# The state part of an update on the whole TensorE array: eight block-diagonal 128x128 matmuls, moved behind the right sides

## The reference

```python
def step(S, inp):                       # two steps for each token
    g, a_t, b_t, k_t, v_t, q_t = inp
    bS = jnp.einsum('bhk,bhkv->bhv', b_t, S)
    S = jnp.exp(g)[..., None] * S + a_t[..., None] * bS[:, :, None, :] + k_t[..., None] * v_t[:, :, None, :]
    o = jnp.einsum('bhk,bhkv->bhv', q_t, S)
    return (S, o)
...
y = out * jax.nn.sigmoid(gate)          # then an RMS norm per head, and y @ Wo
x = _layernorm(x + attention(x))
x = _layernorm(x + x @ W + b + x @ (up_aux @ (lora_up @ (lora_down @ down_aux))))
```

## Time and profile before

| | us |
|---|---|
| median of 3 runs | 2623.15 |
| lowest and highest of them | 2622.76, 2631.74 |
| span of the profiled execution, first to last instruction | 2622.0 |
| TensorE, matmuls busy | 2288.4 (87%) |
| TensorE, weight loads busy | 1721.9 (66%) |
| VectorE busy | 1601.7 (61%) |
| ScalarE busy | 1618.0 (62%) |
| GpSimd busy | 458.8 (17%) |

### The profile page before, as it was taken

The page is one execution under the profiler, slowest core; times in us unless marked ns, Lnnn a source line. Parts: engine busy times, 40 slices in busy tenths (PEclk is TensorE's granted clock), DMA queues, the critical chain, the costliest instruction groups (busy, mean ns, idle before and its releaser), DMA issues.

```text
span 2622.0 us, 225147 instructions
## 1 busy us (share of the span) xinstructions
PE 2288.4 (87%) x102472; PEld 1721.9 (66%) x102472; DVE 1601.7 (61%) x3940; ACT 1618.0 (62%) x3048; POOL 458.8 (17%) x555
## 2 busy tenths in 40 slices
PE   6788898999988899998999998989999988999785
PEld 2556666666666666666676666666666666766573
DVE  2456366666556676656666665666666566666533
ACT  3556466666666666656666666666666666666543
POOL 1011111111111111111111111111111111111210
PEclk7879899999999999999999999999999999999987
DMA  3244455534555554455554455555445555534541
GB/s 95 74 110 121 110 148 148 141 104 127 145 141 151 137 141 111 132 138 146 144 137 118 124 145 146 148 141 142 113 129 143 145 148 148 136 103 132 140 125 41
DMA packets 692934, 338.90 MB, mean 129 GB/s; under 512 B 551794, under 2 KB 651728, under 8 KB 692816
## 3 DMA queue, kind: packets, MB, share of 16 engines
q1 hardware_dynamic: 692816, 337.67, 48.2%
HBM read 35.57 MB, written 16.78 MB: 20 GB/s over the span
## 4 chain that ended last, share of the span: by engine, by line
PE 86%; issue 10%; DVE 2%; ACT 1%; DMA 1%; SPq 0%; ACTq 0%; DVEq 0%
PE bank L570 14%; PE bank L733 13%; PE bank L712 11%; PE bank L704 8%; PE bank L724 7%; PE bank L716 5%; PE bank L593 5%; PE bank L683 5%; PE bank L622 5%; PE bank L643 3%; PE bank L577 3%; PE bank L694 2%; PE bank L602 2%; PE bank L587 2%; PE bank L584 2%
## 5 line engine op out<-in xcount | busy, mean ns | idle before, releaser
L473 POOL TENSOR_TENSOR state<-moved,edge 128x512 f32<-128x512 f32 x252 | 292.3, 1160 | 1821.9 <-DVE moved L1093 1821.9
L712 PE MATMUL bank<-parts,w_now 32*32 32x64 f32 x16512 | 420.1, 223 | 4.8 <-DMA w_now<-w_row 3.6
L570 PE MATMUL bank<-x_col,w_kqv 128*128 128x512 f32 x768 | 370.6, 619 | 48.5 <-issue 47.9
L856 ACT ACTIVATE parts<-bank,cf 128x256 f32<-128x256 f32 x512 | 214.6, 470 | 319.5 <-DVE o_col L1087 310.7
L716 PE MATMUL bank<-aq_now,delta 32*32 32x16 f32 x16512 | 403.7, 179 | 9.2 <-issue 9.2
L716 PEld LDWEIGHTS bank<-aq_now,delta 32*32 32x32 f32 x16512 | 391.7, 110 | 6.7 <-issue 6.7
L712 PEld LDWEIGHTS bank<-parts,w_now 32*32 32x32 f32 x16512 | 377.2, 110 | 17.1 <-issue 5.0
L733 PE MATMUL bank<-uq_now,s_now 32*32 32x24 f32 x32768 | 362.2, 189 | 14.5 <-issue 14.4
L733 PEld LDWEIGHTS bank<-uq_now,s_now 32*32 32x32 f32 x32768 | 337.1, 107 | 24.1 <-issue 18.2
L1116 DVE COPY_PREDICATED aq<-ci,bank 128x128 f32<-128x128 int32 x256 | 77.1, 301 | 410.3 <-PE bank L704 276.7
L1087 DVE TENSOR_TENSOR o_col<-qs,bank 128x64 f32<-128x64 f32 x512 | 89.5, 216 | 388.6 <-PE bank L716 384.7
(11 more groups left out here) (99 smaller groups left out, 3814.1 us busy)
## 6 DMA issues: line engine op xcount, KB each, us to landing
s_now<-state SPq DMA_DIRECT2D x256, 256.0 KB
uq_now<-uqv SPq DMA_DIRECT2D x256, 192.0 KB
t_now<-t_t SPq DMA_DIRECT2D x256, 128.0 KB, 2.0
w_now<-w_row SPq DMA_DIRECT2D x256, 128.0 KB
uq_a<-uqv SPq DMA_DIRECT2D x64, 384.0 KB
low<-uqv SPq DMA_DIRECT2D x64, 384.0 KB
x_col<-in_xt_dram SPq DMA_DIRECT2D x32, 512.0 KB, 5.8
w_a<-w_col SPq DMA_DIRECT2D x64, 256.0 KB
```

The source lines that it names most:

```text
L473: pool.tensor_tensor(state[:, qc, :, :, :].rearrange("p m b v -> p (m b) v"), moved[m % 2][:, :, :, :].rearrange("p m b v -> p (m b) v"), ...
L570: mm = pe.matmul(ps[:, :], w_kqv[:, a, w, f * P:(f + 1) * P], x_col[:, a, :], start=a == 0, stop=a == KT - 1)
L712: pe.matmul(ds_bank[quarter(h), m, :, :].rearrange("p b v -> p (b v)"), w_now[quarter(h), m, :], parts[quarter(h), m, :, :].rearrange("p b ...
L856: act.activation(parts[:, :, b, :], p2_bank, ACT.Copy, scale=cf[:, C_TAKE + b:C_TAKE + b + 1])
```

## The change

Seven edits that belong together:

1. `updates` keeps only the state part. For each of the 8 tiles one matmul with a 128x128 weight, in which the four heads' 32x32 blocks stand on the diagonal and the rest is zero, takes the place of four with 32x32 weights. The 32 answer matmuls become `answers`.
2. A slot runs deltas, answers, right sides, updates. Signals change with it: p3_filled becomes o_filled and ds_filled, the deltas wait for t_now and aq_now (second_in) and for qs, the right sides for first_in, the updates for s_added, w_in and parts_made.
3. w_now becomes [128, 128, 8]: row, weight column, tile. The weight of tile m is w_now[:, :, m], every eighth float. w_row is laid out as [128, chunk, 32, 8] and is written by four transposes with that stride, in place of two contiguous ones.
4. SyncE loads the diagonal with four transfers of 32 partitions by 1 KB (`stage_diagonal`), issued last in the iteration, in place of one of 128 partitions.
5. parts is no longer made by two ScalarE copies from PSUM, but by one GpSimd multiply of delta by the mask columns (`parts_part`), ahead of the decay of the same iteration.
6. inv is cleared and its diagonals set by GpSimd (five memsets) in place of ScalarE's copy of a constant; the constant is gone, and prod shares the space of uq_a's first buffer.
7. VectorE takes the answers first, then turns the right sides, then adds the state.

```diff
             def stage_first(c, n):
 
-                sp.dma_start(uq_now[:, :, :], of_chunks(uqv[c][:, :, 0:HF * UQ], n)).then_inc(uq_in.handle, 16)
-                sp.dma_start(s_now[:, :, :, :], state[:, n % QC, :, :, :]).then_inc(s_in.handle, 16)
+                sp.dma_start(uq_now[:, :, :], of_chunks(uqv[c][:, :, 0:HF * UQ], n)).then_inc(first_in.handle, 16)
+                sp.dma_start(s_now[:, :, :, :], state[:, n % QC, :, :, :]).then_inc(first_in.handle, 16)
+
+            def stage_diagonal(rows, m):
+
+                for h in range(HPH):
+                    sp.dma_start(w_now[quarter(h), quarter(h), :], rows[quarter(h), m, :, :]).then_inc(w_in.handle, 16)
...
+            def parts_part(j, n):
+
+                if not (there(j) and not (isinstance(j, int) and j * CH + n == 0) or (there(j - 1) and n < 1)):
+                    return
+                shape = [P, CT, GB, HD]
+                pool.wait_ge(ds_filled.handle, ds_filled.at(j, n + 1))
+                pool.wait_ge(delta_ready.handle, delta_ready.at(j, n))
+                pool.tensor_tensor(parts[:, :, :, :], delta[:, :, :].unsqueeze(2).to_broadcast(shape),
+                                   cf[:, C_TAKE:C_TAKE + GB].unsqueeze(1).unsqueeze(3).to_broadcast(shape),
+                                   ALU.mult).then_inc(parts_made.handle, 1)
...
             def updates():
 
                 for m in range(CT):
-                    for h in range(HPH):
-                        pe.matmul(ds_bank[quarter(h), m, :, :].rearrange("p b v -> p (b v)"), w_now[quarter(h), m, :],
-                                  parts[quarter(h), m, :, :].rearrange("p b v -> p (b v)"),
-                                  start=True, stop=True)
+                    mm = pe.matmul(ds_bank[:, m, :, :].rearrange("p b v -> p (b v)"), w_now[:, :, m],
+                                   parts[:, m, :, :].rearrange("p b v -> p (b v)"), start=True, stop=True)
+                mm.then_inc(ds_filled.handle, 1)
+
+            def answers():
+
+                for m in range(CT):
                     for h in range(HPH):
                         mm = pe.matmul(o_bank[quarter(h), m, :], delta[quarter(h), m, :], aq_now[quarter(h), m, :],
                                        start=True, stop=True)
-                mm.then_inc(p3_filled.handle, 1)
+                mm.then_inc(o_filled.handle, 1)
...
                 pe.wait_ge(set_up.handle, N_SET_UP)
-                pe.wait_ge(x_turned.handle, turn)
-                pe.wait_ge(t_in.handle, turn16)
-                pe.wait_ge(delta_ready.handle, turn)
-                pe.wait_ge(o_added.handle, turn)
+                pe.wait_ge(second_in.handle, turn32)
+                pe.wait_ge(qs_copied.handle, turn)
                 deltas()
+                answers()
 
                 pe.wait_ge(set_up.handle, N_SET_UP)
-                pe.wait_ge(w_in.handle, turn16)
-                pe.wait_ge(aq_in.handle, turn16)
+                pe.wait_ge(first_in.handle, turn32)
+                right_sides()
+
                 pe.wait_ge(s_added.handle, turn)
+                pe.wait_ge(w_in.handle, turn64)
+                pe.wait_ge(parts_made.handle, turn)
                 updates()
-
-                pe.wait_ge(set_up.handle, N_SET_UP)
-                pe.wait_ge(uq_in.handle, turn16)
-                pe.wait_ge(s_in.handle, turn16)
-                pe.wait_ge(qs_copied.handle, turn)
-                right_sides()
...
             def delta_part(j, n):
 
-                act.wait_ge(p3_filled.handle, p3_filled.at(j, n + 1))
+                act.wait_ge(parts_made.handle, parts_made.at(j, n - 1))
+                act.wait_ge(o_filled.handle, o_filled.at(j, n + 1))
                 act.wait_ge(o_added.handle, o_added.at(j, n - 1))
-                for b in range(GB):
-                    act.activation(parts[:, :, b, :], p2_bank, ACT.Copy, scale=cf[:, C_TAKE + b:C_TAKE + b + 1])
                 act.activation(delta[:, :, :], p2_bank, ACT.Copy).then_inc(delta_ready.handle, 1)
...
                 def turn_part(n):
                     if there(j):
                         turn_right_sides(j, c, n)
+                    add_state(j, n)
```

More of the change, by code:

```diff
@@ L34 @@
 C_TAKE = C_HEADS + P
-C_EYE = C_TAKE + GB
-C_EPS = C_EYE + ROWS * ROWS
+C_EPS = C_TAKE + GB
 C_LOAD = C_EPS + 5
@@ L146, in delta_block @@
         w_col = sb("w_col", [P, TILES, HD])
-        w_row = [sb(f"w_row{c}", [P, TILES, HD]) for c in range(2)]
+        w_row = [sb(f"w_row{c}", [P, CH, HD, CT]) for c in range(2)]
         gate = [sb(f"gate{c}", [P, HF, TOK]) for c in range(2)]
@@ L165, in delta_block @@
         t_now = sb("t_now", [P, CT, HD])
-        w_now = sb("w_now", [P, CT, HD])
+        w_now = sb("w_now", [P, HPH * HD, CT])
         parts = sb("parts", [P, CT, GB, HD])
@@ L381, in iteration @@
                         sp.wait_ge(p2_filled.handle, left)
[L382 to L387, removed]
+                        sp.dma_start(t_now[:, :, :], chunk(t_t, n)).then_inc(second_in.handle, 16)
+                    behind = (there(j) or (there(j - 1) and n < 1)) and not (isinstance(j, int) and j * CH + n == 0)
+                    g, m, own = (j, n - 1, c) if n >= 1 else (j - 1, CH - 1, 1 - c)
+                    if behind:
+                        left, masked = held(sp, first, o_filled.at(j, n + 1)), held(sp, second, aq_masked.at(g, CH))
                         if m == 0:
                             sp.wait_ge(aq_masked.handle, masked)
[L390 to L396, removed]
+                        sp.wait_ge(o_filled.handle, left)
+                        sp.dma_start(aq_now[:, :, :], chunk(aq[own], m)).then_inc(second_in.handle, 16)
                     if there(j) and not (isinstance(j, int) and j == G - 1 and n == CH - 1):
@@ L408, in iteration @@
                         stage_first(0, 0)
+                    if behind:
+                        left, turned = held(sp, first, ds_filled.at(j, n + 1)), held(sp, second, w_turned.at(g, 1))
+                        if m == 0:
+                            sp.wait_ge(w_turned.handle, turned)
+                        sp.wait_ge(ds_filled.handle, left)
+                        stage_diagonal(w_row[own], m)
                     if there(j + 1) and n == 0:
@@ L1088, in update, with add_state @@
                 last.then_inc(o_added.handle, 1)
+            def add_state(j, n):
+                if not scanned(j, n):
+                    return
+                g, m = (j, n - 2) if n >= 2 else (j - 1, CH + n - 2)
+                mine = state[:, m % QC, :, :, :]
+                dve.wait_ge(ds_filled.handle, ds_filled.at(j, n + 1))
                 if isinstance(g, int) and g == G - 1 and m > QC + 1:
@@ L1151, in scan_part @@
                 def scan_part(n):
-                    if there(j) and not (isinstance(j, int) and j * CH + n < 2) or (there(j - 1) and n < 2):
-                        update(j, c, n)
+                    take_answers(j, n)
                 def turn_part(n):
```

86 lines of the change are left out of this document (52 added, 34 removed).

## The result

The changed kernel takes 3618.66 us (median of 4 runs, 3615.04 to 3620.66), the kernel before 2625.88 on the same chip (median of 4, 2622.76 to 2631.74). The ratio is 1.3783 [1.3741, 1.3825]: 38% slower. Forecast was 2716 us with a range up to 2850. The sign was right, the size was not.

The account below looks back on a forecast made before the run. Bound: TensorE's own instructions plus stretches waiting for nothing visible. Per group +2.5 (slots) +0.8 (slot 5) -0.4 (slot 0) = +2.9 us; 32 groups +93; 2622.0 + 1.15 + 93 = 2716 us, own range 2675 to 2770, 80% range 2550 to 2850.

Parts of the forecast that it names:

- 16 x 0.107 = 1.71: New state matmuls on TensorE: 16 load records a slot, spaced 0.107 us apart, take 1.71 us.
- rival 1: Column-strided weight read of w_now costs extra: loads 0.203 us apart, 394 us more, 3110 us; chance 0.15.
- the two products of 0.22: VectorE's solve products: 60 elements read 64 bytes apart take 0.22 us, no more than along the row; evidence against strided cost.
- The slot at the low clock: Slot beginning at 1324.69, at 1.2 GHz: start of deltas to dense work grows by 0.30 us, from 5.39 to 5.69.
- Slot 5's wait: TensorE's second sum of squares waits for the bank that VectorE's first h_row addition drains: stall 0.8 us per group.
- the old wait of 0.45 is covered: -0.4: Slot 0, first scores waiting for uq_a: TensorE arrives 2.3 us late, VectorE 1.8, so 0.4 us per group is saved.
- 1.8 late: VectorE's delay by slot 0: solve tail starts about 1.2 us later in slot 4, plus 0.6 idle in slot 5.
- The issue piece: TensorE's queue walking branches before the dense part, 0.65 us a slot on average: hidden after the change, costed at nothing.
- Rival 3: Issue piece not hidden: a third to all of 0.65 us stays, +55 to +166 us; chance 0.13 shared with Rival 4.
- Rival 2: Loads are not the pace: some 0.055 us a record, -1.9 us per group, 2562 us; chance 0.16.
- Rival 4: w_now lands about 1.3 us late around slots 7 and 0: +42, 2758 us; chance 0.13 shared with Rival 3.
- GpSimd's product: GpSimd's added 128x512 multiply for parts: 1.16 us, done before it is needed, costing nothing; without cover about 1.2 a slot.

Follow-up runs that it names:

- Experiment 2: The changed kernel with weights read at every second or every fourth float of w_now instead of every eighth (wrong numbers, same work): 2853.07 and 3612.57 us.
- Experiment 3: contig with each of the eight state matmuls issued twice in a row: 3257.25 us.
- contig: The changed kernel with w_now and w_row stored tile by tile, so one matmul's 128 weight columns lie side by side: 2877.93 us, ratio to before 1.0971.
- experiment 7: contig with VectorE's state addition moved back, later in iterations 4, 5 and 7: 2788.33 us, ratio to before 1.0608.
- experiment 5: Masked deltas made by two ScalarE copies instead of GpSimd's product: on contig 2797.74 us; with 32x32 state matmuls (quarters_scalar) 2660.83 us.
- experiments 4 to 6: contig with 32x32 state matmuls (2683.95 us; strided weights 2674.52), with ScalarE's masked deltas (2797.74; with 32x32 matmuls too, 2660.83), or with 64x64 state matmuls (2663.65).
- quarters_scalar: contig with the state part as 32 matmuls of 32x32 and the masked deltas made by ScalarE instead of GpSimd: 2660.83 us, ratio to before 1.0137.

## Why the prediction was wrong, step by step

**The step that failed is "16 x 0.107 = 1.71", the spacing of the weight loads.** The prediction took it from two loads of contiguous columns and applied it to columns eight floats apart. It measured 0.25 a record (4.00 a block), more than double. Put into the prediction's own sum, 256 x (4.00 - 1.71) = 586 us: 2716 would have been 3302. This is rival 1, which had a chance of 0.15 and a price of 0.203, taken from ScalarE's 1133 against 597 ns, and 0.25 is dearer than that price too. The argument against it, the two products of 0.22, was VectorE's: another engine, and instructions of 60 elements. It said nothing about a weight load of 128 columns. Experiment 2 shows the mechanism as a step: nearly free at two floats apart, full price at four.

The Trainium skill, "SBUF — State Buffer", section "Door 1: The DMA port swizzle", asks for at least two hits on a 16-byte line. The trace agrees: 215 ns at two hits, 328 to 334 at one. The same place calls floats up to four apart free; the measurement contradicts it for the weight load, where four apart, one hit a line, paid in full (3612.57 us).

**The clock was left out of the sum.** It was taken as 2.4 GHz but for one slot. In the changed kernel it is at 0.50 in much of the dense work, and by the busy times this is most of the 317 us that the corrected 3302 still lacks: removing the stride took 368 us off TensorE's work outside the new matmuls, 67 of which came back as waits. Experiment 3 shows that the block's length alone isn't the cause.

**What is left without the stride** is contig's 162 us above 2716. In one group of its trace the eight slots are 5.6 longer than before, where 2.9 were forecast:
- From the slot's start to dense work 4.52 were forecast; contig shows 1509.52 - 1504.92 = 4.60. Deltas, answers and right sides are 0.65, 0.6 and 1.44 (forecast 0.68, 0.70, 1.33), the block 1.93 for 1.71. With 64 moving columns between them, loads come 0.12 apart, not 0.107.
- The slot at the low clock was given +0.30, on the argument that only the part at its start is slow. Its block takes 3.61 and the dense part 4.48: +1.8. A load at 0.226 where 0.12 is usual was nowhere in the sum.
- Slot 5's wait was forecast as 0.8 and measures 1.32 (from the end of the block at 1532.28 to the end of the addition at 1533.60). Right in place and kind; experiment 7 takes it away.
- Slot 0: "the old wait of 0.45 is covered: -0.4". It became 1.72. The step that failed here is VectorE's "1.8 late". From the start of slot 4 to the end of its last uqv write VectorE took 34.1 us before (1324.69 to 1358.77) and 38.8 in contig (1516.74 to 1555.50): 4.7 late, while TensorE came 3.4 late where 2.3 were forecast. Some 3.3 of the 4.7 lie in single instructions that got longer, which the sum had at nothing, each with GpSimd at work beside it: the four kb_col writes to uqv (2.71 to 3.55), a solve step (0.42 to 1.15), the kb_col product (1.22 to 1.88), a few smaller ones. Contig's last writes, and SyncE's transfer of uq_a right behind them:

```profile
1550.60 3.55 DVE L1320 TENSOR_TENSOR uqv<-kb_col,ep 128x512 f32<-128x512 f32 x4
1554.07 1.43 DVE L1325 TENSOR_TENSOR uqv<-q_col,ep 128x512 f32<-128x512 f32 x2
```

```profile
1549.17 2.76 SPq L365 DMA_DIRECT2D w_now<-w_row  x4
...
1555.57 0.59 SPq L349 DMA_DIRECT2D uq_a<-uqv  x1
```

The mean of such a uqv write rose from 737 ns before to 934 in contig; the last two took 1.43 instead of 1.28. From the issue of uq_a to the first scores it is 3.6 us (1555.57 to 1559.21), as before. Moving the product to ScalarE left that mean at 930 ns; GpSimd's decay still runs there. But it took 0.6 to 0.9 off the wait in slot 0 (experiment 5), so the product has a share in it. That the decay has the rest is an argument from the trace; no run removed it from that place, and the state addition ahead of the q_col writes is not ruled out (experiment 7).

The slots of other groups, which together are 1.7 longer each group than this one (235 us in 32 groups is 7.3), were not itemised.

**What held.** The issue piece is hidden, by the mechanism named: it came back in most slots, at 0.23 to 0.75, as soon as the block fell to 1.1 us (experiments 4 to 6), so contig's 1.9 us of queued matmuls cover it. It gave back some 190 us by the chain's shares, which are rounded to a percent. Rival 3 fell. Rival 2 fell in its own form (contiguous 128-column loads do set the pace), though 64x64 loads reach 0.035 a record. Rival 4 fell: the four w_now issues take 2.76 where 1.9 were forecast, yet TensorE waits on w_now for 6.5 us in all. ScalarE at nothing was right: it holds 1% of the chain as before. The strided w_row transposes cost 1.6 us a group more (124.5 us against 74.5 in all), where some 2 were allowed. GpSimd's product takes 1.04 (forecast 1.16) and was right for GpSimd, but "nothing" left out what it does to VectorE; moving it away gave 58 us, most of them by way of the clock (experiment 5).

## What to carry to other kernels

Before 32x32 matmuls are merged into one on the whole array, look at the stride of the weight operand: small loads that run side by side hide a slow read, and a single large one shows it in full. A duration read on one engine with short instructions is no evidence against a rule for another engine's long ones; when the rows disagree, the range has to reach to the dear one. And an engine that is idle enough to take over work isn't free for its neighbour: ask what that neighbour runs in the same microsecond.

## What was not expected of the hardware

- A weight load of 128 columns with one float in each 16 bytes comes every 0.25 us at both clock levels; with two or four floats in each 16 bytes, every 0.12 to 0.13 at 1.00; contiguous ones come every 0.226 at 0.50.
- During such loads the granted clock falls from 1.00 to 0.58 (1814 to 1816) with TensorE busy all the time, and the next dense part pays (mean clock 0.786; 0.904 with contiguous weights, 0.918 with twice as many of them).
- What was gained by relieving VectorE came mostly with the clock: 42 of 58 us in experiment 5 and 51 of 72 in experiment 7 are TensorE's own busy time, for the same matmuls.
- Two-input fp32 instructions on VectorE lengthen beside GpSimd's: 1.15 us instead of 0.42 for 252 columns, 934 ns instead of 737 for 512 in the mean.
- 64x64 matmuls with 64 moving columns take 0.035 us a record; 128x128 ones take 0.12 for four times the area, and 32x32 ones (quarters_scalar) 1.07 for 64 records, 0.017 each.
